# Last stage of an adaLN/FFN kernel: where two splits, the routing products and the second transposes stand in their queues

## The reference

```python
x = x + L0_ffn(L0_cond(x, ...))      # LoRA linear layer with one adapter per batch, then a gated FFN of width 1376
x = x + L1_ffn(L1_cond(x, ...))      # two linear layers of 512 x 512, each with a top-2-of-8 LoRA mixture
```

```python
logits = x @ Wr.T + bias(language)                 # L1_cond
gates  = softmax over the top 2 of 8
y      = x @ W.T + 2 * sum_e gates[e] * (x @ A[e].T) @ B[e].T
probs  = softmax(y @ W_router.T)                   # L1_ffn
combine = top 2 of 8, divided by their sum
out    = x + y @ W_base.T + b_base + 2 * sum_e combine[e] * (y @ A2[e].T) @ B2[e].T
```

## Time and profile before

| what | value |
|---|---|
| median of 3 runs | 992.07 us |
| the profiled execution, its own time | 994.31 us |
| its span in the trace | 992.6 us |
| PE (matmul) busy | 982.7 us, 99% |
| DVE, ACT, POOL busy | 59%, 47%, 26% |
| HBM read, written | 165.74 MB, 63.44 MB |
| granted TensorE clock | full in all 40 slices |

### The profile page before, as it was taken

The page is one execution under the profiler, slowest core; times in us unless marked ns, Lnnn a source line. Parts: engine busy times, 40 slices in busy tenths (PEclk is TensorE's granted clock), DMA queues, the critical chain, the costliest instruction groups (busy, mean ns, idle before and its releaser), DMA issues.

```text
span 992.6 us, 14042 instructions
## 1 busy us (share of the span) xinstructions
PE 982.7 (99%) x4787; PEld 830.4 (84%) x4787; DVE 586.8 (59%) x969; ACT 464.9 (47%) x854; POOL 256.0 (26%) x244
## 2 busy tenths in 40 slices
PE   9999999999999999999999999999999999999998
PEld 7888888878888888888888888888888998888876
DVE  5654586777784323596423398333377587785762
ACT  4645567555661333572333373233356273535342
POOL 5242232654400631400532230261140450000000
PEclk9999999999999999999999999999999999999999
DMA  8997866666977877867887777986688740615222
GB/s 287 334 327 281 309 216 245 240 231 236 340 265 260 283 229 193 274 222 267 287 278 193 233 249 248 321 279 192 192 293 285 254 166 28 228 61 194 78 93 85
DMA packets 121486, 230.12 MB, mean 232 GB/s; under 512 B 12612, under 2 KB 12612, under 8 KB 121160
## 3 DMA queue, kind: packets, MB, share of 16 engines
q1 hardware_dynamic: 118880, 220.81, 66.5%
q0 software_dynamic: 2400, 8.41, 2.3%
q10 hardware_dynamic: 136, 0.01, 0.0%
HBM read 165.74 MB, written 63.44 MB: 231 GB/s over the span
## 4 chain that ended last, share of the span: by engine, by line
PE 96%; DVE 1%; ACT 1%; issue 1%; DMA 0%; SPq 0%; ACTq 0%; DVEq 0%
PE bank L1820 95%; PE bank L1844 1%; PE bank L1981 1%; DMA w_raw<-in_w 0%; ACT xs_hi L1126 0%; ACT bank L1277 0%; DVE hg L1644 0%; DVE t_lo L1535 0%; DVE greater L1624 0%; ACT res L1285 0%; DVE diff L1601 0%; DVE top L1597 0%; DVE wins L1620 0%; DVE rank L1627 0%; DVE greater L1618 0%
## 5 line engine op out<-in xcount | busy, mean ns | idle before, releaser
L1820 PE MATMUL bank<-cop_hi,wring 128*128 128x512 f32 x1234 | 380.8, 389 | 0.9 <-ACT bank L1041 0.9
L1820 PEld LDWEIGHTS bank<-cop_hi,wring 128*128 128x128 f32 x1234 | 231.8, 188 | 49.4 <-ACT bank L1041 1.3
L1820 PE MATMUL bank<-cop_lo,wring 128*128 128x512 f32 x616 | 239.8, 389 | 0.0
L1820 PE MATMUL bank<-op_hi,wring 128*128 128x512 f32 x560 | 173.8, 389 | 0.0
L1472 DVE TENSOR_TENSOR v<-bank,p7s 128x512 f32<-128x512 f32 x44 | 30.4, 692 | 204.6 <-PE bank L1820 204.6
L1820 PEld LDWEIGHTS bank<-cop_lo,wring 128*128 128x128 f32 x616 | 115.7, 188 | 23.8
L1820 PEld LDWEIGHTS bank<-op_hi,wring 128*128 128x128 f32 x560 | 105.2, 188 | 21.7
L1820 PE MATMUL bank<-op_lo,wring 128*128 128x512 f32 x280 | 109.0, 389 | 0.0
L1072 ACT ACTIVATE s<-bank 128x512 f32<-128x512 f32 x44 | 26.3, 598 | 117.9 <-PE bank L1820 117.8
L1458 DVE TENSOR_TENSOR op_lo<-h,op_hi 128x512 fp32r<-128x512 f32 x100 | 72.9, 747 | 3.3 <-ACT op_hi L1029 3.1
L821 POOL TENSOR_TENSOR h_t<-h,h 128x512 f32<-128x512 f32 x20 | 27.7, 1385 | 161.1 <-DVE h L1494 161.1
(11 more groups left out here) (227 smaller groups left out, 1931.4 us busy)
## 6 DMA issues: line engine op xcount, KB each, us to landing
wring<-wgu_scratch SPq DMA_DIRECT2D x231, 256.0 KB, 3.1
wring<-wd_scratch SPq DMA_DIRECT2D x140, 256.0 KB, 4.9
wgu_scratch<-wring SPq DMA_DIRECT2D x77, 256.0 KB, 3.5
x_raw<-in_x SPq DMA_DIRECT2D x32, 256.0 KB, 6.2
c_scratch<-c_out SPq DMA_DIRECT2D x32, 256.0 KB, 2.9
c<-c_scratch SPq DMA_DIRECT2D x32, 256.0 KB, 4.6
xs_raw<-x_scratch SPq DMA_DIRECT2D x16, 512.0 KB, 6.2
out<-res SPq DMA_DIRECT2D x32, 256.0 KB, 2.1
```

What stands on the lines that cost most here:

```text
L1820: return e.matmul(out_ap, lhs, rhs, start=start, stop=stop, skip_group_check=True)
```

## The change

Four things move; nothing is added, removed or resized, and the programs of ACT, POOL and SyncE are the same row for row.

1. DVE: the split of half a tile of unit 1, `split_x2(1, 0, 0)`, stood in front of `router(0, 1)`. It now stands behind `turn_h(0, 0)`.
2. DVE, units 0, 1 and 2: `route_h(a + 2)` stood in front of the splits of T3 and T2, and now stands behind them.
3. PE, units 1 and 2: the routing products of the two next tiles stood behind product 3 of the first half. They now stand in front of it. In unit 0 they keep their place.
4. PE, all units: `turn_h(1, b)`, the transposes of the second tile, stood behind `out_h1(…, "c12")`. They now stand in front of it.

```diff
@@ dve_program
         split_s(4)
-        split_x2(1, 0, 0)
         router(0, 1)
         split_t(0, 1)
         turn_h(0, 0)
+        split_x2(1, 0, 0)
         route_h(0)
@@ dve_program
                 turn_h(0, a + 2)
-                route_h(a + 2)
                 split_t(u + 1, 3)
                 split_t(u + 1, 2)
+                route_h(a + 2)
@@ pe_program
-                if mp == 0 and more:
-                    route_x(a + 2)
-                    route_x(b + 2)
+                    if mp == 0 and more and i == (3 if u == 0 else 4):
+                        route_x(a + 2)
+                        route_x(b + 2)
                 out_h1(u, mp, "c11")
                 out_h1(u, mp, "c21")
@@ pe_program
                 out_h1(u, mp, "c22")
-                out_h1(u, mp, "c12")
                 if mp == 0:
                     turn_h(1, b)
+                out_h1(u, mp, "c12")
```

## The result

| | before | after |
|---|---|---|
| median | 992.07 us (991.67 to 994.35, 5 runs) | 988.09 us (987.22 to 988.70, 5 runs) |
| the profiled execution, its own time | 994.31 us | 988.70 us |
| its span | 992.6 us | 986.9 us |

The ratio of after to before is 0.9955, with a 95% interval of 0.9941 to 0.9970: 3.0 to 5.9 us faster. The forecast was 988.1 us, 4.0 us faster. That the median agrees to a hundredth of a microsecond is luck, with an interval 2.9 us wide.

What follows compares the result with a forecast made beforehand. PE, busy 99% of the span, was taken as the bound, so only its holes could be won. Moves 1, 3, 4 and 2 summed as -1.0 + 0.28 - 1.1 - 2.2 = -4.0 us, from 992.07 to 988.1 us; range 986.7 to 990.0.

Steps and rivals of the forecast that it cites:

- 1 (no new wait): Second tile's routing products, units 1 and 2: no new wait for their splits; 986.5 us, chance 0.13.
- 2 (issue, or late loads): Product 5's hole is really "issue", or T splits wait for loads, delaying `route_h(6)`; 989.1 to 990.3 us, chance 0.17.
- 3 (holes refilled): On PE, each hole could be refilled one instruction later, so nothing measurable changes; about 992 us, chance 0.06.
- 4 (DVE falls behind): Routing products, units 1 and 2: DVE's splits 3.2 us later make the kernel slower, 994.5 us; chance 0.04.

Runs made afterwards that it cites:

- routing products split: The changed kernel with only the first tile's routing products in front of product 3 in units 1 and 2, the second tile's behind it; ratio to before 0.9937.

## Why the prediction was right, point by point

| term | predicted | stage length, move alone | its places in the changed kernel |
|---|---|---|---|
| move 1 | -1.0 | -0.97 | -0.98 |
| move 3 | +0.28 | +0.17 (1.75 less the clock's 1.58) | +0.17 |
| move 4 | -1.1 | -1.07 | -1.05 |
| move 2 | -2.2 | -2.14 | -2.09 |
| sum | -4.0 | -4.01 | -3.95 |

- **Move 1** rested on laying an "issue" wait to DVE, because DVE's split ended 0.10 us before PE went on. The kernel with this move alone confirms it.
- **Move 3** was forecast to win nothing, as a trade of a wait for a wait. Both sides are in the trace, and sending only the first tile's products ahead removes both, worth some 1 us.
- **Move 4**: right in sum, with one part mis-sized. In unit 3 I had 0.10 us of gain (0.30 removed, 0.2 new). The new wait is 0.28 us, and with move 4 alone unit 3 wins 0.05; units 0 to 2 win 0.34, 0.35 and 0.31, where I had 0.36, 0.30 and 0.30.
- **Move 2**: the splits fit in the idle time, but with less to spare than forecast. In the result's trace ACT waited 0.38 us for the load of its second `t_raw`, DVE waited 0.21 us for the `t_hi` made from it, and `route_h(6)` started 0.20 us later than before, counted from the first matmul behind PE's `turn_h(0, 6)` (5.08 us after it, 4.88 before); the forecast allowed 0.1. In the second trace of the change the load was on time and `route_h(6)` not later (4.88). Product 7 came 0.50 and 0.43 us behind product 1, so there the two traces differ by 0.07 only, and the 0.2 to 0.3 us of wait left there is what was forecast.
- **The restart.** Move 4 closes holes of 0.28 + 3 x 0.19 = 0.85 us and opens one of 0.28, a net 0.57, and the stage wins 1.07. Most of what stands over is the slow restart behind each wait: the second matmul came 0.08, 0.11, 0.10 and 0.10 us late at the four closings before, and the matmul behind the waiting transposes 0.03 late after, which makes 0.93. The other 0.14 is within what stage lengths resolve. PE's weight loads at the second closing c22 of unit 1, before, show where the restart comes from:

```profile
888.91 0.19 PEld L1820 LDWEIGHTS bank<-hg_hi,b_lo 128*128 128x128 f32 x1
889.56 0.19 PEld L1820 LDWEIGHTS bank<-hg_hi,b_hi 128*128 128x128 f32 x1 [0.46 <-DVE hg_lo L1653]
889.67 0.19 PEld L1820 LDWEIGHTS bank<-hg_lo,b_hi 128*128 128x128 f32 x1
```

The load at 888.91 starts 0.23 us ahead of its matmul (889.14). Behind the wait the first load starts with its matmul (889.56), and the second 0.11 us later; its matmul follows at 889.90, again 0.23 behind it and thus 0.34 behind the first. The Trainium skill's rule that weight loads are pulled ahead of running matmuls (TensorE: Matmul & The Clock Gate, "Step-by-step: what each phase is for") does not carry across a wait here, as the rows of before had it.
- **Rivals.** 1 (no new wait) is out: the wait stands in the trace of the change, in its second one, and with move 3 alone. 2 (issue, or late loads) is out as a loss of 1 us or more with move 1 alone and move 2 alone; a late load there was in one trace of the change, of a few hundredths of a us at product 7. 3 (holes refilled) is out by the stage lengths. 4 (DVE falls behind) did not happen; that a us of DVE is a us of PE was shown at product 7, not at the routing products, where it was not tried.
- **What I had not priced** is the clock. The forecast took the hole of 2.09 us at its own length. In the runs of the result it seems to have made little difference (3.98 us between the medians, 3.95 in the stage; the clocks of the runs of before are not listed there). On the two chips of the experiments half of the executions of before have a lowered mean and are 2 us longer, some 1 us on average, and there the medians of before and the change lie 5.9 us apart. By those medians, and by their ratio (5.1 us), a forecast of 4.0 us less would have been 1 to 2 us too small there; this term would give 1 us of it.

## What to carry to other kernels

Where one engine is busy 99% of the time, read its holes from start to start, follow each to the instruction that ends it, and ask what stands in front of that instruction in its own queue; work that stands there and could run while that engine idles is the gain. A block moved forward brings its own waits forward with it: compare each of its operands' ready times with the new start, and if only its second half is late, move only the first half. To judge changes of one microsecond in a millisecond, compare a stretch of the trace from one marked instruction to another, since the untouched stages alone vary by more.

## What the runs showed of the hardware

- **A wait of 2 us on TensorE can cost nearly as much again.** In half of the executions with the 2.1 us hole (49 of 98) the mean clock was lower by 0.002 or more; in the one that was traced the granted clock was 1.00 through the hole (955 to 957 us), fell to its lower level 0.6 us after the engine had started again, and stayed there for about eight matmuls: 1.58 us lost. Without the hole it was 1 of 35. The Trainium skill (TensorE: Matmul & The Clock Gate, "What's actually happening") says that half clock is the idle engine's state and activity releases it; the trace agrees on the two levels. Executions with a mean of 0.999 exist without this hole too. One was traced (routing products split): its granted clock is 1.00 from 982 to 984 us and 0.69 from 984 to 985, behind the last matmul (981.96), where it costs PE nothing.
- **"issue" is not always the engine's own.** The 0.78 us laid to it at product 5 were DVE's, as move 1 alone shows. The new wait at the transposes of unit 3 is laid to "issue" too, and most likely is DVE's as well: in all six traces that have it, the transposes start 0.15 us after `hg` ends. No run moved `hg` to prove it.
